# Second attention of a three-part transformer kernel: one output bank, division after the weighing, jobs across batch borders

## The reference

```
q, k, v = xn @ Wq, xn @ Wk, xn @ Wv        # xn: normed input
q, k = rope(q), rope(k)                    # rotary over the 8 columns of a head
s = q k^T + rel_emb[bucket(i - j)]         # causal, 256 x 256 for each head
o = softmax(s) v
x = x + norm(o @ Wo)
```

## Time and profile before

| what | value |
|---|---|
| median of three runs | 2417.43 us |
| the profiled execution's own time | 2419.39 us |
| its span | 2417.5 us |
| TensorE busy in the span | 2280.3 us (94%) |
| VectorE busy | 1755.6 us (73%) |
| ScalarE busy | 1379.3 us (57%) |
| GpSimd busy | 1596.8 us (66%) |
| first scores of the second attention | 1814.54 us |
| last addition into X there | 2130.03 us |

### The profile page before, as it was taken

One profiled execution on the slowest core, in us unless ns is written; L12 is line 12 of the kernel. 1 busy time (PEld: TensorE's weight loads), 2 busy tenths in 40 slices (PEclk: granted clock), 3 DMA queues, 4 the chain that ended last, 5 costly groups with the idle time before them and its releaser, 6 DMA issues.

```text
span 2417.5 us, 81630 instructions
## 1 busy us (share of the span) xinstructions
PE 2280.3 (94%) x34944; PEld 1563.9 (65%) x34944; DVE 1755.6 (73%) x2707; ACT 1379.3 (57%) x2778; POOL 1596.8 (66%) x931
## 2 busy tenths in 40 slices
PE   7789999999999999999999999999968888889998
PEld 5456666666666666666666666666646666656665
DVE  3678887888788878887888788878838888822322
ACT  2256666666666666666666666666626666633332
POOL 1298888898889888988898889888912322101111
PEclk9899999999999999999999999999979999989999
DMA  4011112111221112111221112211130000000000
GB/s 115 3 38 36 33 35 66 44 34 33 57 53 34 34 31 70 42 34 32 54 58 34 31 36 60 52 32 35 35 113 1 1 1 1 1 1 5 5 5 5
DMA packets 77303, 83.91 MB, mean 35 GB/s; under 512 B 24964, under 2 KB 48786, under 8 KB 76946
## 3 DMA queue, kind: packets, MB, share of 16 engines
q1 hardware_dynamic: 76946, 78.70, 12.7%
HBM read 26.56 MB, written 1.07 MB: 11 GB/s over the span
## 4 chain that ended last, share of the span: by engine, by line
PE 62%; DVE 20%; issue 10%; ACT 5%; POOL 3%; SPq 0%; ACTq 0%; DMA 0%; POOLq 0%; DVEq 0%
PE bank L564 8%; PE bank L645 7%; PE bank L657 6%; DVE n L1266 5%; PE lnbank L585 4%; PE obank L634 4%; ACT qk L941 3%; PE bank L575 3%; PE obank L626 3%; PE sbank L601 3%; PE bank L665 3%; PE bank L856 3%; PE obank L611 3%; PE obank L866 2%; PE sbank L866 2%
## 5 line engine op out<-in xcount | busy, mean ns | idle before, releaser
L1259 DVE TENSOR_TENSOR qk<-bank,tab 128x1024 f32<-128x1024 f32 x384 | 468.7, 1221 | 194.7 <-ACT qk L941 194.6
L1577 POOL TENSOR_TENSOR rn<-n2m,cst 128x16 f32<-128x16 f32 x192 | 562.8, 2931 | 16.0
L1573 POOL TENSOR_TENSOR qk<-qk 128x1024 f32<-128x1024 f32 x192 | 454.6, 2368 | 156.9 <-DVE qk L1259 156.9
L564 PE MATMUL bank<-wqk,xs 128*128 128x512 f32 x768 | 405.0, 609 | 1.7 <-DVE qk L1259 0.9
L941 ACT ACTIVATE qk<-bank 128x512 f32<-128x512 f32 x384 | 226.9, 591 | 314.0 <-PE bank L564 314.0
L1581 POOL TENSOR_TENSOR qk<-qk,rn 128x1024 f32<-128x1024 f32 x192 | 365.4, 1903 | 28.1 <-POOL rn L1577 0.9
L575 PEld LDWEIGHTS bank<-cst,qk 128*128 128x128 f32 x1536 | 191.5, 141 | 215.3 <-issue 170.7
L575 PE MATMUL bank<-cst,qk 128*128 128x128 f32 x1536 | 231.8, 274 | 11.0 <-POOL qk L1581 11.0
L1266 DVE TENSOR_REDUCE n<-qk 128x16 f32<-128x1024 f32 x192 | 232.1, 1209 | 0.0
L1585 POOL TENSOR_TENSOR lnr<-lnv,cst 128x2 f32<-128x2 f32 (+1 forms) x76 | 54.3, 714 | 244.1 <-DVE lnv L1143 244.1
L585 PE MATMUL lnbank<-wv,xs 128*64 128x512 f32 x768 | 208.0, 620 | 0.0
(11 more groups left out here) (357 smaller groups left out, 4231.0 us busy)
## 6 DMA issues: line engine op xcount, KB each, us to landing
vp<-vp SPq DMA_DIRECT2D x672, 65.0 KB, 2.0
wqk<-in_L_ffn_Wqkv SPq DMA_DIRECT2D x24, 256.0 KB, 3.6
wv<-in_L_ffn_Wqkv SPq DMA_DIRECT2D x6, 512.0 KB, 3.9
wo<-in_L_ffn_Wo SPq DMA_DIRECT2D x6, 512.0 KB, 4.2
xs<-Z SPq DMA_DIRECT2D x48, 64.0 KB, 2.4
xs<-Z SPq DMA_DIRECT2D x48, 63.8 KB, 2.1
vp<-in_L_ffn_w SPq DMA_DIRECT2D x1, 2048.0 KB, 13.7
mw<-in_L_ffn_w SPq DMA_DIRECT2D x8, 256.0 KB, 6.8
```

The source lines that it names most:

```text
L564: nc.tensor.matmul(bank[s % 2][:, :], xs[:, odd, WIN + r * P:WIN + r * P + P], wqk[:, lo:lo + 512], start=True, stop=True).then_inc(p_full, 1)
L1259: tt(qk[:, both, :].rearrange("p o (h d) -> p o h d", d=DH), heads(bank[c % 2][:, :]).unsqueeze(1).broadcast_to([P, 2, PAIRS, DH]), table. ...
L1573: tt(direct, direct, swapped, ALU.add).then_inc(sum_done, 1)
L1577: tt(rn[:, m % 2, :], n2m[:, :], const("mhalf"), ALU.pow).then_inc(rn_done, 1)
```

## The change

Six things are changed together.

1. A *group* of three jobs (y = 0 to 3) now holds heads y, y + 4, y + 8 and y + 12. Those lie in four different strips of 32 rows, so scores are computed for all four at once: `scores3` contracts over 32 rows for each head, with queries masked four ways instead of sixteen, into four banks (`quad`), each strip into its own. There is one set of these banks.
2. VectorE adds the bias, negates and reduces in one `tensor_tensor_reduce` for each head (`shift3`). ScalarE's exponential has scale -1. Three buffers instead of two hold these.
3. The exponentials are weighed undivided (`weigh3`). All 16 heads of a batch add up into 256 columns of one bank: `placed` picks a 32-column slice of the values in which the head's 8 columns stand at its place, with zeros around them.
4. Division comes after: `invert` takes the 32 reciprocals, two transposes spread them (`spread_inverses`), ScalarE copies the sum out (`take_raw`) and VectorE multiplies 256 columns (`divide3`). `out3` is one matmul.
5. Steps have 12 slots. Jobs are numbered over batch borders: a batch's last turns and weighings stand in slots 0 to 2 of the next step. ScalarE's queue within a slot is exponentials, copy of the turned weights, `finish`, `prepare` (before: copy, exponentials, `prepare`, `finish`).
6. `bias` has its own buffer and is loaded after layer 0 of the stage before; `mw2` lies in the buffers of `kT` and `tab` and is loaded where the bias was. Four small loads of `Wo` become one and a memset goes.

```diff
-JOBS = [job for n in range(0, H, 4)
-        for job in ((0, range(n, n + 4)), (1, range(n, n + 2)), (1, range(n + 2, n + 4)))]
+JOBS = [job for y in range(4)
+        for job in ((0, range(y, H, 4)), (1, range(y, H // 2, 4)), (1, range(H // 2 + y, H, 4)))]
...
             load_xs(0, 0, 0)
             layer(0, True, False)
+            sp.dma_start(bias[:, :, :], bass.AP(relu_dram.ap().tensor, 0, [[1, P], [384, H], [1, S]])).then_inc(rel_in, 16)
...
             def out3(b):
-                pe.wait_ge(s3["ot"], 2 * b + 2)
-                for g in range(4):
-                    mm = nc.tensor.matmul(lnbank[:, 0:S], s3wo[:, g, :], s3ot[:, g, :], start=(g == 0), stop=(g == 3))
-                mm.then_inc(s3["y"], 1)
+                pe.wait_ge(s3["ot"], b + 1)
+                nc.tensor.matmul(lnbank[:, S:2 * S], s3wo, s3ot, start=True, stop=True).then_inc(s3["y"], 1)
...
+            def scores3(b, odd, y):
+                if y == 0:
+                    pe.wait_ge(s3["qk"], 2 * b + 2)
+                    pe.wait_ge(s3["qm"], b + 1)
+
+                wait(pe, s3["mx"], NJ * b + 3 * y)
+                for r in range(2):
                     w = P * (r + 1)
+                    for g in range(4):
+                        rows = slice(WIN * g, WIN * g + WIN)
+                        mm = nc.tensor.matmul(quad[:, g, P * r:P * r + w], qm[rows, odd, y, r * P:r * P + P],
+                                              s3k[odd][rows, 0:w], start=True, stop=True)
+                mm.then_inc(s3["full"], 1)
...
+            def weigh3(n):
...
+                lo = r * P
+                for kb in range(r + 1):
+                    for x, h in enumerate(heads):
+                        row, q = WIN * (h // 4), x * (r + 1) + kb
+                        mm = nc.tensor.matmul(bank[b % 2][row:row + WIN, lo:lo + P], placed(b % 2, kb, h),
+                                              pT[:, n % 2, q * P:q * P + P], start=(m == 0), stop=(y == 3 and kb == r),
+                                              skip_group_check=True)
+                mm.then_inc(s3["pv"], 1)
+
+            def spread_inverses(b):
+
+                pe.wait_ge(s3["rdb"], b + 1)
+                pe.wait_ge(s3["raw"], b + 1)
+                for r in range(2):
+                    mm = nc.tensor.transpose(bank[b % 2][:, r * P:r * P + P], rdw[:, b % 2, r * P:r * P + P], ident)
+                mm.then_inc(s3["rdw"], 1)
 
             def step3(b, odd, next_batch, batch_before):
                 u = 3 * b + (LN_S3 + 1)
-                for m in range(NJ + 3):
-                    attend(b, odd, m)
+                for m in range(NJ if next_batch else NJ + 4):
+                    n = NJ * b + m
+                    if 2 <= n <= NJ * B + 1:
+                        turn3(n - 2)
+                    if m in (2, 5, 8):
+                        scores3(b, odd, m // 3 + 1)
+                    if m == NJ - 1 and next_batch:
+                        scores3(b + 1, 1 - odd, 0)
+                    if 3 <= n <= NJ * B + 2:
+                        weigh3(n - 3)
                     if next_batch:
                         prepare(b + 1, m, u if batch_before else LN_S3 + 2)
                     if batch_before:
-                        finish(b - 1, m, u + 2 if next_batch else u, next_batch)
+                        finish(b - 1, m, u + 2 if next_batch else u)
+                    if m == 3 and batch_before:
+                        spread_inverses(b - 1)
+                    if m == 15:
+                        spread_inverses(b)
...
+                for x, h in enumerate(heads):
+                    last = nc.vector.tensor_tensor_reduce(out=s3sh[n % 3][:, x * w:x * w + w], in0=quad[:, h // 4, P * r:P * r + w],
+                                                          in1=bias[:, h, S - w:S], scale=-1.0, scalar=3e38, op0=ALU.add,
+                                                          op1=ALU.min, accum_out=mx[:, n % 3, x:x + 1])
+                last.then_inc(s3["mx"], 1)
+
+            def invert(b):
+                dve.wait_ge(s3["px"], NJ * b + NJ)
+                nc.vector.reciprocal(rdn[:, b % 2, :], dn[:, b % 2, :]).then_inc(s3["rdn"], 1)
+                dve.wait_ge(s3["rdn"], b + 1)
+                wait(dve, s3["rdw"], b - 1)
+                nc.vector.tensor_copy(rdw[:, b % 2, :].rearrange("p (h d) -> p h d", d=HD),
+                                      rdn[:, b % 2, :].unsqueeze(2).broadcast_to([P, 2 * H, HD])).then_inc(s3["rdb"], 1)
+
+            def divide3(b):
+
+                dve.wait_ge(s3["rdw"], b + 1)
+                wait(dve, s3["y"], b)
+                tt(s3ot.rearrange("p (r t) -> p r t", r=2), s3raw.rearrange("p (r t) -> p r t", r=2),
+                   bank[b % 2][:, 0:S].rearrange("p (r t) -> p r t", r=2)[:, :, ::-1], ALU.mult).then_inc(s3["ot"], 1)
```

More of the change, by code:

```diff
@@ L167, in build @@
         w1t = rotf[:, 512:1024]
-        mw2 = sb("mw2", [P, NE, 4, DIM])
+        bias = sb("bias", [P, H, S])
         sh = sb("sh", [P, 2, 512])
@@ L834, in _ @@
             step3(B - 1, 1, False, True)
-            for slot in range(9, 13):
-                finish(B - 1, slot, LN_S4 - 1, False)
+            for slot in range(8, 12):
+                finish(B - 1, slot, LN_S4 - 1)
             pe.wait_ge(ld_gate, 64)
@@ new lines, in exps3 @@
+            def exps3(b, m):
+                n = NJ * b + m
+                r, heads = JOBS[m]
+                w = P * (r + 1)
+                act.wait_ge(s3["mx"], n + 1)
+                wait(act, s3["ptf"], n - 2)
+                if m == 0:
+                    wait(act, s3["rdn"], b - 1)
+                for x, h in enumerate(heads):
+                    last = nc.scalar.activation(s3px[n % 3][:, x * w:x * w + w], s3sh[n % 3][:, x * w:x * w + w], ACT.Exp,
+                                                bias=mx[:, n % 3, x:x + 1], scale=-1.0,
+                                                accum_out=dn[:, b % 2, H * r + h:H * r + h + 1])
+                last.then_inc(s3["px"], 1)
@@ L1078, in step3, with take_raw @@
+            def take_raw(b):
+                act.wait_ge(s3["pv"], NJ * b + NJ)
+                wait(act, s3["ot"], b)
+                nc.scalar.copy(s3raw.rearrange("p (r t) -> p r t", r=2),
+                               bank[b % 2][:, 0:S].rearrange("p (r t) -> p r t", r=2)[:, :, ::-1]).then_inc(s3["raw"], 1)
             def step3(b, odd, next_batch, batch_before):
                 u = 3 * b + (LN_S3 + 1)
-                for m in range(NJ + 3):
-                    attend(b, m)
+                for m in range(NJ if next_batch else NJ + 3):
+                    n = NJ * b + m
+                    if m < NJ:
+                        exps3(b, m)
+                    if 2 <= n <= NJ * B + 1:
+                        take_turned3(n - 2)
+                    if batch_before:
+                        finish(b - 1, m, u + 2 if next_batch else u)
```

224 lines of the change are left out of this document (88 added, 136 removed).

## The result

The changed kernel takes 2403.86 us (median of 4 runs, 2402.7 to 2405.35) against 2418.11 us: a ratio of 0.9941, 95% interval 0.9924 to 0.9958. It is faster by 14.3 us, and the prediction said 35.

A forecast was written before the change was run, and what follows sets the result against it. TensorE and VectorE, each busy 32.8 of 38.6 us a step, were near their limit, neither at it. A walked step of 34.55 us saves 29.8 over seven steps, the last 4.9: 34.7 less, 2383 us; range 2350 to 2420.

The forecast's parts named there:

- A group of scores: TensorE's scores of three jobs on four strips: 1.0 us taken, between 0.8 side by side and 3.1 one after another.
- rival 3: Strips run one by one, everything behind the scores stands 3.1 instead of 1.0 us: slower, 2449 us; chance 0.08.
- the walk: One second-attention step followed queue by queue, from one batch's first scores to the next's: 34.55 us, against 38.8 before.
- The fused instruction: VectorE's addition and maximum in one, with accumulator read: 1.3 us a job of one key block, 0.95 of two.
- Rival 2: VectorE's fused instruction takes two cycles a column: a step of 37.4 us, 2405 us; chance 0.08.
- rival 5: The 2 MB bias load is not hidden, up to 10 us once: 2393 us; chance 0.04.
- four segments: The step's path in four parts, each ending with a group's scores: 8.65, 8.55, 9.55 and 7.8 us.
- rival 4: TensorE's clock: busy share falls from 85% to 78%, half clock a third of the time adds 3.5: 2407; chance 0.06.
- exponentials 1.65, copy 0.55, weighing 0.55: Part of the step's path: ScalarE's exponentials, then its copy of turned weights, then TensorE's weighing directly, in us.
- The last step: The last batch, walked without a next batch: 37.3 us instead of 42.2, a gain of 4.9.
- Rival 1: Looser queues: most of VectorE's charged waiting is hidden, a step of about 29.5 us, 2344 us; chance 0.12.
- so a copy that is ready stands behind them: ScalarE does a job's exponentials ahead of the copy of older turned weights; no size of its own given.

The follow-up runs named there:

- a4: The changed kernel with two extra matmuls of 256 columns, which nobody reads, ahead of the turn in slots 1, 4, 7 and 10: 2392.24 us (0.9902).
- a1: The changed kernel with ScalarE's copy of the turned weights put back ahead of the job's exponentials: 2351.07 us (0.9731).
- a8: The changed kernel with addition and maximum as two passes again, plus two unread matmuls in slots 1, 4, 7 and 10: 2425.63 us (1.0031).
- c4: The changed kernel with copy first, two banks for turned weights, norm matmuls ahead of the weighing, and the added unread matmuls: 2336.13 us (0.9655).

## Why the prediction was wrong

**What held.** A group of scores, sixteen rows, takes 0.94 us at full clock (forecast 1.0), where the same work took 3.1 us before, so the strips run side by side and rival 3 fell. The 1.0 us of the walk was my estimate between 0.8 us side by side and 3.1 one after another: no run shows that term, and the runs showed 0.94 in its place. The fused instruction is cheaper than forecast: 3 x 0.34 + 4 x 0.18 = 1.7 us a step to the good. It takes 0.42 us for 256 columns, with one source in PSUM, and that is what a plain addition takes. Rival 2 fell. X additions went to 0.42 us, and the bias load is hidden (rival 5 fell). The walk's four segments, 8.65, 8.55, 9.55 and 7.8 us, were met closely in a4's step at full clock: 8.63, 8.62, 9.71 and 8.21. So is the sum of seven steps: a4's first (31.42 us, at a clock of 0.85), its second (33.50) and five times 35.17 are 240.8 us, where seven times 34.55 are 241.9. But both are met by luck, because two errors cancel.

**The steps that failed.** The first is in the sum: it walks every step at the full clock, and puts the clock at nothing outside rival 4. The changed kernel ran its seven steps in 257.9 us, 16 more than the forecast, and by the estimate above the clock has some 17 of them. TensorE idles behind ScalarE's late copy, in spells such as the 2.63 us, and its clock is 0.89 in the last five steps.

The second is hidden in the path: the walk's "exponentials 1.65, copy 0.55, weighing 0.55". It knew that the copy stands behind the exponentials, and let the weighing follow the copy at once (in the first and last of its four segments even the square, 0.45 and 0.4 us). In TensorE's queue the turn of another job comes first, waits for the same copy, and takes 0.63 us (the chain of the changed kernel). Four turns and two weighings of 0.56 us, less the two squares, are 2.8 us a step; terms that were set a little too high take some of it back. The account of a step:

| | us a step |
|---|---|
| forecast | 34.55 |
| fused instruction cheaper | -1.74 |
| rest up to a4's step at full clock, mainly turns and weighings | +2.4 |
| a4's step at full clock | 35.17 |
| clock (estimate) | +2.3 |
| measured, mean of the last five steps | 37.5 |

With the two shorter steps ahead of them the mean of all seven is 36.85.

**The last step** takes 43.4 for 37.3 us, 6.1 more. Its last exponentials end 31.0 us after the first scores (forecast 25.9), with the same wait for the copy and a mean clock of 0.85. In a4 it takes 41.5 us (2060.89 to 2102.36) at a clock of 0.91, so that 2 of the 6.1 or more are the clock's. In a1, with the copy first, it is 36.5 (2027.22 to 2063.69), a little under the walk. 16.1 and 6.1 are 22.2 us; the first scores came 1.8 us earlier than before (1812.77 for 1814.54), and the miss was 20.9.

**Rivals.** Rival 4, the clock, was given 0.06 and 24 us (2407 for 2383) as a case of its own; by the estimate it came true at some 19 of them, and the time that it named, 2407 us, was 3 off. The sign for it was the share of busy time in a step: TensorE had 85% at a granted clock of 1.00 before, and has 74% at 0.89 in the last five steps of the changed kernel (139.35 of 187.38 us). Its chance was far too small. Rival 1 (looser queues, 29.5 us a step, 2344 us) is near what the kernel becomes once the copy is first: 29.88 us in a step at full clock, 30.8 in the mean, 2351 us.

**What was not priced.** The prediction gives ScalarE's new order half a sentence ("so a copy that is ready stands behind them"), without a term, a rival or a bound. The walk has the copy behind the exponentials from the start and was never made with the copy ahead of them, so that its cost could not show. That half sentence held 53 us, more than the whole gain forecast.

What stays open: where in a slot the added matmuls do their good, how much of the 53 us of the late copy is the clock's, and the combination that was not run (copy last, fused, the rest as before).

## What to carry to other kernels

When a producer writes into a single buffer, try the instruction that empties it first in its engine's queue, ahead of a job's long pieces, or give the producer a second buffer. Price each reordering by itself, in both kernels if they can be had; here one swap cost between 40 and 68 us and hid most of what the other parts had brought. And where TensorE's busy share falls, forecast its clock too (here 0.98 before and 0.90 after between 1850 and 2050 us, at 171 and 147 us of work): compare the granted clock of the stage before and after, and try work that nobody needs.

## What the runs showed of the hardware

- In the changed kernel the accumulator's read costs VectorE next to nothing between two fused instructions: starts are 0.21 us apart at 128 columns and 0.34 at 256, though the instructions last 0.28 and 0.42 and the reads 0.08; behind a plain instruction of 256 columns, without a read, the next starts after 0.33.
- A group of eight fp32 matmuls (sixteen rows of the profile) on four strips of 32 rows takes 0.94 us at a granted clock of 1.00 and 1.66 at 0.50, where the same work on the whole array took 3.1 at 1.00: 3.3 times.
- Matmuls without use made three kernels faster, by 11.6 (a4), 33.9 (a8) and 9.8 us (c4), the last one with TensorE busy for 95% of a step once they were in; the granted clock between 1850 and 2050 us went from 0.90 to 0.93, 0.76 to 0.91 and 0.97 to 0.98.
